# Row maxima of attention scores: one reduction and one signal for each bank of 512 columns

## The reference

```
logits = einsum('bhqd,bhkd->bhqk', q, k) * scale          # q, k after rotary embedding
probs  = softmax(logits + causal_mask, axis=-1)
L      = eye(s) - tril(probs, -1)
rhs    = diagonal(probs)[..., None] * v
A      = solve_triangular(L, rhs, lower=True)
out    = A.transpose(0, 2, 1, 3).reshape(b, s, HID) @ Wd.T + bd
```

## Time and profile before

| what | value |
|---|---|
| median of 3 timed runs | 2480.72 us |
| lowest, highest | 2473.66, 2480.91 us |
| profiled execution | 2477.26 us |
| its span, first to last instruction | 2475.5 us |
| mean granted TensorE clock | 0.663 of 2.4 GHz |

### The profile page before, as it was taken

How to read it: one execution, slowest core, us unless ns; L and a number is a source line. 1 busy time by engine, 2 the same in 40 slices (tenths; PEclk the granted TensorE clock), 3 DMA queues, 4 the chain that set the end, 5 groups by cost and what they waited for, 6 DMA issues and landing times.

```text
span 2475.5 us, 50097 instructions
## 1 busy us (share of the span) xinstructions
PE 1635.3 (66%) x21864; PEld 1120.6 (45%) x21864; DVE 1756.6 (71%) x3727; ACT 547.5 (22%) x787; POOL 217.9 (9%) x138
## 2 busy tenths in 40 slices
PE   1566426666787677777877885665757575757565
PEld 1343314444454444444534563453636454545445
DVE  6564367778857766777687547969686877777777
ACT  1100111222232323333333441202021211112120
POOL 9000011111111111101001110000000000000000
PEclk7667555555555655556566666787868686868687
DMA  3042942222012220110220130000000000000000
GB/s 120 0 102 61 156 98 50 50 51 51 25 34 51 50 44 15 44 44 30 30 44 15 32 92 22 1 1 5 1 5 1 5 5 1 5 1 5 1 5 5
DMA packets 130220, 84.02 MB, mean 34 GB/s; under 512 B 100690, under 2 KB 118100, under 8 KB 125524
## 3 DMA queue, kind: packets, MB, share of 16 engines
q1 hardware_dynamic: 130004, 80.85, 14.6%
HBM read 31.54 MB, written 49.28 MB: 33 GB/s over the span
## 4 chain that ended last, share of the span: by engine, by line
DVE 47%; PE 34%; issue 11%; SPq 2%; POOL 2%; DMA 2%; ACT 1%; DVEq 0%; ACTq 0%; POOLq 0%
DVE mraw L1157 8%; DVE zb L1205 6%; DVE tb L1200 6%; DVE hoty L1337 5%; PE pb L951 5%; DVE r L1336 4%; PE pb L973 4%; PE pb L965 3%; PE pb L847 3%; PE pb L798 2%; PE pb L867 2%; DVE hotx L1333 2%; PE pb L877 1%; DVE iv L1268 1%; PE pb L943 1%
## 5 line engine op out<-in xcount | busy, mean ns | idle before, releaser
L1157 DVE TENSOR_REDUCE mraw<-pb 128x2 f32<-128x1024 f32 (+3 forms) x304 | 354.5, 1166 | 174.3 <-PE pb L803 128.8
L798 PE MATMUL pb<-kall,qa 48*128 48x512 bf16 (+3 forms) x768 | 166.8, 472 | 241.0 <-DVE mraw L1157 191.9
L965 PE MATMUL pb<-r,hoty 128*128 128x64 bf16 x3072 | 139.8, 219 | 238.9 <-DVE su L1348 193.4
L613 ACT ACTIVATE et<-pb 128x1024 f32<-128x1024 f32 x224 | 228.5, 1024 | 310.6 <-PE pb L814 309.1
L965 PEld LDWEIGHTS pb<-r,hoty 128*128 128x128 bf16 x3072 | 133.9, 115 | 246.3 <-DVE su L1348 197.6
L1200 DVE TENSOR_TENSOR tb<-cst,zb 128x31 f32<-128x31 f32 (+15 forms) x496 | 194.9, 393 | 66.7 <-POOL cst L542 54.1
L1205 DVE TENSOR_TENSOR zb<-zb,tb 128x31 f32<-128x31 f32 (+15 forms) x496 | 197.9, 399 | 13.5
L847 PE MATMUL pb<-et,a_all 128*9 128x128 f32 x3584 | 203.2, 366 | 2.5 <-ACT et L613 1.9
L798 PEld LDWEIGHTS pb<-kall,qa 48*128 48x128 bf16 x768 | 38.0, 109 | 303.2 <-DVE mraw L1157 241.7
L814 PE MATMUL pb<-qm,kall 50*128 50x128 bf16 x2304 | 159.3, 282 | 0.7 <-ACT ed L613 0.7
L1337 DVE TENSOR_TENSOR hoty<-iyb,iotab 128x4096 bf16<-128x4096 bf16 x32 | 141.4, 4417 | 0.0
(11 more groups left out here) (182 smaller groups left out, 2450.0 us busy)
## 6 DMA issues: line engine op xcount, KB each, us to landing
ed_d<-ed SPq DMA_DIRECT2D x32, 1024.0 KB, 4.6
cst<-ed_d SPq DMA_DIRECT2D x128, 64.0 KB, 4.9
qs_d<-qkp SPq DMA_DIRECT2D x48, 128.0 KB, 2.3
ks_d<-qkp SPq DMA_DIRECT2D x48, 128.0 KB, 2.3
qa<-qs_d SPq DMA_DIRECT2D x64, 96.0 KB, 2.6
kall<-ks_d SPq DMA_DIRECT2D x8, 672.0 KB, 21.6
xin<-L_attn_hidden_states SPq DMA_DIRECT2D x4, 512.0 KB
out<-xs SPq DMA_DIRECT2D x8, 256.0 KB, 2.2
```

Source lines behind the costliest of these rows:

```text
L613: nc.scalar.activation(dst, src, ACT.Exp, scale=SCALE).then_inc(s["exp_done"], 1)
L798: last = mm(place, qa[64 * hh:64 * hh + KR, par, bb, g0 + m, :], kall[64 * hh:64 * hh + KR, batch(s_, bb), g0 + m, c0:c0 + w], start=True, ...
L965: last = mm(spread_w(q)[:, j].rearrange("p c g -> p (c g)"), hoty[:, n % 2, at, :], r4[:, part, n % 2, at, :, :].rearrange("p c g -> p (c ...
L1157: V.reduce_max(mraw[:, bb, :, g0:g0 + count, c0 // 512], pb[0][:, :].rearrange("p (e n) -> p e n", e=2)[:, :, 0:count * w].rearrange("p e ...
```

## The change

On TensorE the matmuls of a unit are ordered by row half: all of hh = 0 with their masks, a signal, then all of hh = 1 with their masks, a signal. Each half waits only for the reduction of its own bank. On VectorE the one reduction over both banks becomes two, each of one bank, each with its own wait and its own signal. Both semaphores count two for a unit.

```diff
@@ TensorE: max_job
-                if k:
-                    if jobs[k - 1][0] == "unit":
-                        pe.wait_ge(s["max_red"], units_of[k])
-                    else:
-                        pe.wait_ge(s["qm_ready"], turns_of[k])
+                behind_unit = k > 0 and jobs[k - 1][0] == "unit"
+                if k and not behind_unit:
+                    pe.wait_ge(s["qm_ready"], turns_of[k])
...
-                for m in range(count):
-                    for hh in range(2):
-                        place = pb[0][:, hh * 512 + m * w:hh * 512 + (m + 1) * w]
-                        last = mm(place, qa[64 * hh:64 * hh + KR, par, bb, g0 + m, :], kall[64 * hh:64 * hh + KR, batch(s_, bb), g0 + m, c0:c0 + w],
-                                  start=True, stop=not last_block, skip_group_check=True)
-                if last_block:
+                for hh in range(2):
+                    if behind_unit:
+                        pe.wait_ge(s["max_red"], 2 * units_of[k] - 1 + hh)
                     for m in range(count):
-                        for hh in range(2):
+                        last = mm(pb[0][:, hh * 512 + m * w:hh * 512 + (m + 1) * w], qa[64 * hh:64 * hh + KR, par, bb, g0 + m, :],
+                                  kall[64 * hh:64 * hh + KR, batch(s_, bb), g0 + m, c0:c0 + w], start=True, stop=not last_block, skip_group_check=True)
+                    if last_block:
+                        for m in range(count):
                             last = mm(pb[0][:, hh * 512 + (m + 1) * w - P:hh * 512 + (m + 1) * w], identb[:, :], maskb[:, :], start=False, stop=True, skip_group_check=True)
-                last.then_inc(s["max_lg"], 1)
+                    last.then_inc(s["max_lg"], 1)
@@ VectorE: max_job
-                v.wait_ge(s["max_lg"], units_of[k] + 1)
-                V.reduce_max(mraw[:, bb, :, g0:g0 + count, c0 // 512], pb[0][:, :].rearrange("p (e n) -> p e n", e=2)[:, :, 0:count * w].rearrange("p e (m n) -> p e m n", n=w),
-                             AX.X).then_inc(s["max_red"], 1)
+                for hh in range(2):
+                    v.wait_ge(s["max_lg"], 2 * units_of[k] + hh + 1)
+                    V.reduce_max(mraw[:, bb, hh, g0:g0 + count, c0 // 512], pb[0][:, hh * 512:hh * 512 + count * w].rearrange("p (m n) -> p m n", n=w),
+                                 AX.X).then_inc(s["max_red"], 1)
                 if u < len(max_units(s_)) - 1:
                     return
-                v.wait_ge(s["max_red"], units_of[k] + 1)
+                v.wait_ge(s["max_red"], 2 * units_of[k] + 2)
```

## The result

The changed kernel takes 2523.4 us (median of 4 runs, 2521.7 to 2525.1) against 2477.8 of before on the same chip. The ratio is 1.0185, with an interval of 1.0164 to 1.0207: **46 us slower**. I had forecast 2498 us and a range to 2520. The direction was right and the size was half of what came.

A forecast was written before the change was run, and what follows sets the result against it. Neither engine alone sets the time; VectorE and TensorE wait for each other at the `pb[0]` hand-over. 11 + 18 + 2 - 10 = +21 us on 2477.3 gave 2498 us; range 2470 to 2520, the forecast's own 2488 to 2508.

The forecast's parts named there:

- second reduction: VectorE in the attention stage: two half-reductions for one cost 0.07 us in each of 154 units, +11 us.
- matmuls by row half: TensorE, masked units: halves run one behind the other, 0.6 us more in each of 30 units, +18 us.
- split waits and what VectorE gains: Unit hand-over: later second halves cost +2 us; shorter VectorE waits, mostly ending at the next unit, give -10 us.
- The rival that they do not overlap: VectorE's half-reductions: each pair costs the full 154 ns more, +39 us in all, 2516 us; chance 0.12.
- 154 units: Units without a VectorE wait, 119 and 59, less 24 whose next unit finds VectorE waiting; charged +11 us.
- the step that failed: Masked units on TensorE: longer matmuls cost nothing where TensorE waits for VectorE at the next unit, 0 us.
- The 30 units that I charged: Masked units from 488 us on where TensorE does not wait, next unit of the same kind: 0.6 us each, +18 us.
- the 92 that I called hidden: Masked units whose next unit found TensorE waiting for the reduction: serial order taken as hidden, 0 us.
- The gain that goes through: Rival at the 54 units where both engines wait: all 23 us are kept, 2468 us; chance 0.20.
- The clock: Rival in the attention stage: TensorE's granted clock rises, 13 us back, +8 us, 2485 us; chance 0.23.
- signs of being wrong: Masked units keeping pace near 1390 us, `esub` waits shrinking much more than 4 us, or attention-stage clock above 0.6.
- my own rival: Attention stage: TensorE's clock rises, 164 us more at 2.4 GHz giving 13 us back; chance 0.23.

The follow-up runs named there:

- e2: Kernel before with two reductions a unit, one per bank; matmuls still alternating, one signal from TensorE, one wait on each side: 2497.1 us.
- e3: Changed kernel with the masks of a unit moved behind the scores of both halves: 2489.1 us.
- e8: Kernel before, split with masks last only in single-head-pair units of even half slots and the unit ahead of each: 2481.9 us.
- e10: Changed kernel without its split waits: order by row half and two reductions, but one wait on each side and one signal for both halves: 2582.0 us.
- e6: Changed kernel, but TensorE waits once, in front of the unit, for both reductions of the unit before; each half keeps its signal: 2534.7 us.

## Why the prediction was wrong

The steps e2, e3 and the changed kernel give each term of my sum its measured counterpart, in my own order of the terms:

| term | forecast, us | measured, us | from |
|---|---|---|---|
| second reduction | +11 | +17 | e2 |
| matmuls by row half | +18 | +36 | change less e3 |
| split waits and what VectorE gains | +2 - 10 | -7 | e3 less e2 |
| sum | +21 | +46 | |

So 18 of the 25 us that I was off lie in the second line. The last two measured terms are uncertain by some 9 us each.

*The second reduction.* The overlap was right: a pair takes 1.28 us where the one operation of the earlier trace rows took 1.22, and in 200 of the 304 units the second half starts some 0.08 us before the first ends. The rival that they do not overlap is out: it would have made a pair 1.37 us (2 x 0.685). The Trainium skill, VectorE: DVE Perf Modes, in the section on the DRAIN, says that the next operation starts only when the pipe is empty, and that one which is not held starts earlier. This pair behaves as in that exception, by 0.08 us. The count was off. I charged 154 units; the 17 us of e2 fit a share for each of the 304.

*The matmuls by row half.* The cost of a masked unit was right to 0.03 us. The Trainium skill, TensorEngine Tiling (Array Packing), in Tiling Modes, Key Properties, says that to change the tiling mode drains TensorE. The rows here fit this, though they cannot show a drain as such: from the scores to the masks it is 0.53 to 0.56 us, where the 512 columns alone make 0.43 at 1.2 GHz (an estimate, 512 / 1.2 GHz) and the plain pair of the earlier trace rows took 0.40 to the next work. The new order has three such changes inside a unit instead of one. The exposure was wrong, and this is **the step that failed**: "Where TensorE waits for VectorE at the next unit, this is hidden, since those waits are long". The waits were not long enough, and where they end with the reduction they hide nothing. With one wait and one signal the order costs 86 us, not 18. The 30 units that I charged make 18 of it, the 92 that I called hidden 32. The remaining 54 masked units were not tried alone. If the shares add, they have the rest, 36 us, for which I gave no reason and no cost; that they have it is not shown. In the trace of before 48 of them leave VectorE less than 0.6 us, and the same sum as for the 92 makes 25 us for them. In the changed kernel itself the masks' place is worth 36 us (e3), twice the 18.

*The two waits.* I gave -10 + 2 for the pair. The 7 us between e2 and e3 and the +3 of e8 are in keeping with a gain that mostly ends at the next unit, within their noise; no run shows by itself where it ends. What I missed is that VectorE's early first half also hides a part of the serial second half, 44 us of it (e10 to e6). So, counted from the order alone, two sizes were missed: a cost by 68 us and a repair by 46 us. What is left, 22 us, and 6 us of the second reduction make up the error of 25 us within 3. That the forecast was off by no more than 25 us is in part luck, since the two misses point opposite ways.

*The rivals.* The gain that goes through did not come. The clock did not rise: at 2.4 GHz the attention stage had 164 us before and 109 us after, though TensorE was busier.

*Signs and ranges.* One of my own signs of being wrong came: a fall of the waits for `esub` by much more than 4 us. They fell from 76 to 55 us. With the order alone they are 64 us, with the masks behind both halves 74 and with VectorE's own waits split beside the serial order (e6) 47. So the fall goes with the longer units and with VectorE's early first half, and it is no gain of the whole. My range of 2488 to 2508 us also does not follow from its terms: +8 to +30 on 2477.3 us is 2485 to 2507.

## What to carry to other kernels

In a hand-over between two engines, time that an engine waits in front of a step is poor cover for making that step longer, when the wait ends with the other engine's work: here 32 of some 55 us that such waits were to hide were paid. A longer step needs room in two places. Its result must have lain ready for that long before someone took it, and the engine itself must have waited for that long before its next step. And before loops are reordered so that each half can be signalled, look whether the old order ran the halves side by side on the array; here a matmul over all 128 rows between them ended that (0.89 to 1.53 us a unit), and the split signals and waits won back 54 of the 100 us that the serial halves and the second reduction cost.

## What was not expected of the hardware

The granted clock of the attention stretch fell from 0.57 to 0.54 while TensorE's busy time in it rose from 805 to 911 of 1140 us. In the faster kernel with two inverse operations it was 0.59 at 799 us busy. The fall goes with the serial halves and not with the split: with the order alone it is 0.54, with the split and the masks behind both halves 0.57. On the whole the longer kernels have the lower clock (over the whole span 0.669 at 2462 us, 0.663 at 2475, 0.645 at 2523 and also at 2579), though not one by one (0.650 at 2534 us). No run here separates cause from effect, so a share of each cost above may be the clock's. At the rate of my own rival (13 us for 164 us more at 2.4 GHz) the 55 us less would be some 4 of the 46 us, an estimate. That stays open. Serial halves keep one half of the array's rows at work at a time and take twice as long, which the busy share counts as more work.
